# Row-group pairs of score and maxima products in a two-layer gated attention kernel, with gathers and scatters issued one at a time in the first half of a step

## The reference

```python
x = x + tanh(g_xattn[0]) * L0_xattn(layernorm(x), ctx, mask1)   # no biases but bo, mask per (query, key)
x = x + tanh(g_ffn[0])   * L0_ffn(layernorm(x))                 # 8 experts, the best 2 of each row, exact gelu
x = x + tanh(g_xattn[1]) * L1_xattn(layernorm(x), ctx, ctx, mask2)  # with biases
x = x + tanh(g_ffn[1])   * L1_ffn(layernorm(x))                 # fft, sparse complex product, ifft, bias
```

## Time and profile before

| | us |
|---|---|
| median of 3 executions | 1349.95 |
| lowest, highest | 1343.78, 1759.76 |
| the profiled execution | 1340.18, span 1338.6, mean granted clock 0.944 |

### The profile page before, as it was taken

How to read it: one execution, slowest core, us unless ns; L and a number is a source line. 1 busy time by engine, 2 the same in 40 slices (tenths; PEclk the granted TensorE clock), 3 DMA queues, 4 the chain that set the end, 5 groups by cost and what they waited for, 6 DMA issues and landing times.

```text
span 1338.6 us, 35030 instructions
## 1 busy us (share of the span) xinstructions
PE 1210.1 (90%) x11816; PEld 1001.9 (75%) x11816; DVE 890.7 (67%) x2695; ACT 570.9 (43%) x1187; POOL 261.6 (20%) x374
## 2 busy tenths in 40 slices
PE   4898999988869999899998999999997999999996
PEld 3777777777658888688886888888874777777784
DVE  4787767777647675565856676766565777777763
ACT  4565555545423232422324242422233555555462
POOL 5024334233320000000000000000022334433310
PEclk9998978878779999999999999999997999999998
DMA  9544324334434021131301212101122222222200
GB/s 294 169 129 145 125 89 139 105 113 152 153 127 147 32 92 59 48 105 36 126 31 59 95 56 88 40 29 37 39 65 66 64 72 87 77 75 70 86 29 24
DMA packets 82755, 119.67 MB, mean 89 GB/s; under 512 B 27325, under 2 KB 52557, under 8 KB 80588
## 3 DMA queue, kind: packets, MB, share of 16 engines
q1 hardware_dynamic: 64172, 60.32, 14.6%
q0 software_dynamic: 12848, 49.05, 11.2%
q10 hardware_dynamic: 5616, 8.78, 1.8%
HBM read 63.81 MB, written 47.58 MB: 83 GB/s over the span
## 4 chain that ended last, share of the span: by engine, by line
PE 77%; DVE 8%; issue 7%; ACT 2%; SPq 2%; ACTq 2%; DMA 1%; POOL 0%; DVEq 0%; POOLq 0%; another core or an unknown queue 0%
PE bank L1758 25%; PE bank L1771 13%; PE bank L1519 7%; PE bank L1585 7%; PE bank L1441 5%; PE bank L1572 3%; PE bank L1504 3%; PE bank L1502 3%; PE bank L1461 3%; PE bank L1525 2%; PE bank L1596 1%; PE bank L1545 1%; PE bank L1583 1%; DVE bm L1081 1%; PE bank L1487 1%
## 5 line engine op out<-in xcount | busy, mean ns | idle before, releaser
L1758 PE MATMUL bank<-tiles,we 128*128 128x256 f16 (+1 forms) x3744 | 395.3, 259 | 5.9 <-issue 5.0
L1758 PEld LDWEIGHTS bank<-tiles,we 128*128 128x128 f16 x3744 | 326.1, 98 | 47.5 <-issue 13.5
L935 ACT ACTIVATE tiles<-bank 128x256 f32<-128x256 f32 (+1 forms) x312 | 109.5, 354 | 336.0 <-PE bank L1758 302.5
L1771 PE MATMUL bank<-we,tiles 128*128 128x256 f16 x1608 | 224.8, 274 | 20.9 <-DVE tiles L1372 20.0
L1368 DVE SCALAR_TENSOR_TENSOR tiles<-bank,tiles 128x256 f32<-128x256 f32 (+1 forms) x312 | 120.1, 385 | 165.7 <-ACT tiles L935 161.6
L1771 PEld LDWEIGHTS bank<-we,tiles 128*128 128x128 f16 x1608 | 148.2, 98 | 58.3 <-DVE tiles L1372 33.7
L1081 DVE TENSOR_REDUCE bm<-bank 128x4 bf16<-128x308 f32 x256 | 116.5, 475 | 78.7 <-PE bank L1504 62.9
L1519 PE MATMUL bank<-qT,kbd 128*128 128x256 f16 x960 | 166.7, 294 | 2.4 <-issue 1.4
L471 DVE TENSOR_TENSOR pr<-pr 128x512 f16<-128x512 f32 x160 | 108.5, 682 | 35.2 <-ACT pr L797 32.7
L1374 DVE TENSOR_TENSOR tiles<-tiles 128x256 f16<-128x256 f32 (+1 forms) x312 | 121.1, 388 | 12.1 <-DVE tiles L1372 1.7
L1519 PEld LDWEIGHTS bank<-qT,kbd 128*128 128x128 f16 x960 | 99.1, 106 | 24.8 <-issue 3.0
(11 more groups left out here) (197 smaller groups left out, 1693.3 us busy)
## 6 DMA issues: line engine op xcount, KB each, us to landing
expert_out<-zeros SPq DMA_DIRECT2D x16, 896.0 KB
wes<-in_guT POOLq DMA_DIRECT2D x9, 1024.0 KB, 5.1
tiles<-expert_in SPq DMA_DIRECT2D x29, 256.0 KB, 2.6
pr<-in_guT POOLq DMA_DIRECT2D x7, 1024.0 KB
yg<-in_dnT POOLq DMA_DIRECT2D x7, 1024.0 KB
expert_out<-tiles ACTq DMA_DIRECT2D x28, 256.0 KB, 2.1
expert_in<-zeros POOLq DMA_DIRECT2D x8, 640.0 KB, 12.8
xin<-in_x SPq DMA_DIRECT2D x16, 256.0 KB
```

What stands on the lines that cost most here:

```text
L935: act.activation(ge[:, fc % 2, 0:n * P], bank[1 + fc % 3][:, 0:n * P], ACT.Gelu, scale=INV).then_inc(s.gelu, 1)
L1758: last = pe.matmul(bank[1 + fc % 3][:, half * S:half * S + w * P], gate_up[:, par, c, i, col:col + P], xT[:, j, c, 0:w * P], start=n == 0, ...
L1771: last = pe.matmul(bank[4 + t][:, 0:D], act16[:, fc % 4, i, t * P:(t + 1) * P], we[:, par, 2, j, fc * D:(fc + 1) * D], start=fc == 0 and n ...
```

## The change

Chunks: the 616 columns of a half are cut so that chunks 0 and 1 hold columns 0 to 255 (heads 0 to 3, partitions 0 to 63), chunks 2 and 3 columns 360 to 615 (heads 4 to 7, partitions 64 to 127), and `REST` the columns 256 to 359, which cross. Group 0 is the two rest chunks at full height (`scores_rest`). Groups 1 and 2 (half c=0), and 3 and 4 (c=1), are made together: four mask products first, then the key products two by two, one on partitions 0 to 63 for one group and one on 64 to 127 for the other, into different banks. The maxima products likewise go in pairs (`top_pair`), over four banks instead of two. The exponentials read two banks at once. The order of all queues is rewritten: TensorE has all scores before `values`, ACT all exponentials before `q_hi`, DVE `w_low(b, 1)` ahead of `residual` and `w_low` 3 and 4 ahead of the maxima. The scatters handle batch b-3 instead of b-2; scatter or gather 0 follows the mask copy, 1 and 2 the copy `a_hi`, 3 the first root. `recall` comes one step earlier, at the step's end, for which `slots` gets a 17th column. The number of matrix products and of transfers is the same.

```diff
+REST = 4
+CHUNKS = (0, P, ROWS - 2 * P, ROWS - P, (ROWS - P) // 2)
 NCH = len(CHUNKS)
 GS = KC * NCH // 2
+GROUPS = (((0, REST), (1, REST)), ((0, 0), (0, 1)), ((0, 2), (0, 3)), ((1, 0), (1, 1)), ((1, 2), (1, 3)))
 NW = 8
...
-        bank = [ctx.enter_context(nc.psum_tensor(f"bank{i}", [P, 512], F32)) for i in range(8)]
+        banks = [ctx.enter_context(nc.psum_tensor(f"bank{i}", [P, 2, 512], F32)) for i in range(4)]
+        bank = [banks[i // 2][:, i % 2] for i in range(8)]
...
-        def a_place(g):
-            return b_top[:, 0:4 * S2] if g % 2 == 0 else b_small[:, 0:4 * S2]
+        def a_place(b, g):
+            if isinstance(b.i, int) and b.i == 0:
+                return bank[(5, 2)[g % 2]][:, 0:4 * S2]
+            return bank[(5, 2, 3, 4)[g % 4]][:, 0:4 * S2]
...
+        def score_place(g, j):
+            if g == 0:
+                return bank[3][:, j * S:(j + 1) * S]
+            return banks[(0, 2, 3, 1, 2)[g]][:, j, 0:S]
...
-                late = b.layer == 0 and not (isinstance(b.i, int) and b.i < 2)
+                late = b.layer == 0 and not (isinstance(b.i, int) and b.i < 3)
+                part = ld and b.layer == 1
+                one = (lambda n: gather(b.after(3), n)) if part else (lambda n: scatter(b.after(-3), n))
+                if part:
+                    wait_apart(pool, s.places_recalled, b.i + 4)
+                if late:
+                    scatter_ready(b.after(-3))
+                if late or part:
+                    wait_apart(pool, s.mask_ready, b.n + 1)
+                    one(0)
+                    if tail:
+                        wait_apart(pool, s.attended_high, pv.n + 1)
+                    one(1)
+                    one(2)
                 if tail:
                     ln_root(1, s.root_after, s.variance_after, pv)
+                if late or part:
+                    one(3)
                 if pre:
                     root(b.after(2))
-                if ld and b.layer == 1:
-                    gather(b.after(3))
-                if late:
-                    for t in range(QT):
-                        scatter(b.after(-2), t)
+                if b.layer == 0 and isinstance(b.i, int) and b.i == 15:
+                    scatter_ready(b.after(-2))
+                    for n in range(2 * QT):
+                        scatter(b.after(-2), n)
...
+                expo(b, 0)
                 if tail:
                     a_hi(pv)
-                expo(b, 0)
                 expo(b, 1)
+                expo(b, 2)
                 if front:
                     h_hi(nx)
-                expo(b, 2)
                 expo(b, 3)
+                expo(b, 4)
                 if front:
                     q_hi(nx)
                 if tail:
...
                     v_spread(nx, 0)
                 if tail:
                     tail_out(pv)
-                expo(b, 4)
...
-                if ld and b.layer == 1:
-                    recall(b.after(3))
                 if pre and b.layer == 0:
                     mask_flags(b.after(2))
                 w_low(b, 0)
+                w_low(b, 1)
                 if tail:
                     residual(pv)
-                w_low(b, 1)
                 w_low(b, 2)
                 if b.layer == 0 and not (isinstance(b.i, int) and b.i < 2):
                     place(b.after(-2))
...
                     renorm(pv)
                 if pre:
                     pre_stats(b.after(2))
+                w_low(b, 3)
+                w_low(b, 4)
                 if front:
-                    q_low(nx)
                     maxima(nx, 0)
                     maxima(nx, 1)
+                    q_low(nx)
                     maxima(nx, 2)
                     maxima(nx, 3)
-                w_low(b, 3)
-                if front:
-                    maxima(nx, 4)
                 if pre:
                     pre_norm(b.after(2))
                 if front:
+                    maxima(nx, 4)
                     maxima(nx, 5)
-                w_low(b, 4)
-                if front:
                     maxima(nx, 6)
                     maxima(nx, 7)
                 if tail:
...
                         route(pv, 0)
                     else:
                         finish(pv)
+                if ld and b.layer == 1:
+                    recall(b.after(4))
                 normalise(b)
...
+            def top_pair(b, k):
+                t, c = k // KC, k % KC
+                if k == 0:
+                    pe.wait_ge(s.queries_high, b.n + 1)
+                    pe.wait_ge(s_kbd[b.par], 16 * HC * (b.half + 1))
+                    pe.wait_ge(s.mask_ready, b.n)
+                elif k > 1:
+                    pe.wait_ge(s.maxima, b.n * GP + 2 * (k - 1))
+                for u in range(2):
+                    pe.matmul(a_place(b, 2 * k + u), identb[:],
+                              bm[:, t, 0:S2].unsqueeze(1).to_broadcast([P, 4, S2]), start=True, stop=False)
+                for u in range(2):
+                    rows64 = slice(u * 64, (u + 1) * 64)
+                    last = pe.matmul(a_place(b, 2 * k + u), qT[rows64, b.par, 0, c, t * P:(t + 1) * P],
+                                     kbd[rows64, b.par, 0, c, 4 * u:4 * u + 4], start=False, stop=True)
+                    last.then_inc(s.top_scores, 1)
...
+            def score_keys(b, ki, c, chunk):
+                flat = kbd[:, b.par, ki, c].rearrange("p h k -> p (h k)")[:, CHUNKS[chunk]:CHUNKS[chunk] + P]
+                return flat if chunk == REST else flat[chunk // 2 * 64:chunk // 2 * 64 + 64]
+            def masked(g, j, start):
+                c, chunk = GROUPS[g][j]
+                first = c * ROWS + CHUNKS[chunk]
+                keys = mhead[:].rearrange("p h k -> p (h k)")[:, first:first + P]
+                return pe.matmul(score_place(g, j), keys, mrhs[:], start=start, stop=not start)
+            def scores_rest(b):
+                pe.wait_ge(s.queries_low, b.n + 1)
+                pe.wait_ge(s_kbd[b.par], 16 * HC * (b.half + 1))
+                for j in range(2):
+                    c = GROUPS[0][j][0]
                     for n, (ki, qi) in enumerate(PASSES):
+                        pe.matmul(score_place(0, j), score_keys(b, ki, c, REST), qT[:, b.par, qi, c],
+                                  start=n == 0, stop=False)
+                    if j == 0:
+                        pe.wait_ge(s.mask_ready, b.n + 1)
+                    last = masked(0, j, False)
+                last.then_inc(s.scores, 1)
+            def scores(b, c):
+                g = 1 + 2 * c
+                if c == 0:
+                    if isinstance(b.i, int) and b.i == 0:
+                        pe.wait_ge(s.bulk_low, NU * (b.layer + 1))
+                else:
+                    pe.wait_ge(s.weights, b.n * GS + 2)
                 for j in range(2):
+                    for u in range(2):
+                        masked(g + u, j, True)
+                for j in range(2):
+                    for n, (ki, qi) in enumerate(PASSES):
+                        for u in range(2):
+                            rows64 = slice(u * 64, (u + 1) * 64)
+                            last = pe.matmul(score_place(g + u, j), score_keys(b, ki, c, 2 * u + j),
+                                             qT[rows64, b.par, qi, c], start=False, stop=n == 2)
+                            if j == 1 and n == 2:
+                                last.then_inc(s.scores, 1)
...
-                    pe.wait_ge(s.values_spread, KC * b.n + 1)
-                    if isinstance(b.i, int) and b.i == 0:
-                        pe.wait_ge(s.bulk_low, NU * (b.layer + 1))
+                    pe.wait_ge(s.values_spread, KC * b.n + 2)
+                    pe.wait_ge(s.weights, b.n * GS + 3)
...
                 nx, pv = b.after(1), b.after(-1)
+                scores_rest(b)
+                if tail:
+                    t_att(pv)
                 scores(b, 0)
-                if tail:
-                    pe.wait_ge(s.values_spread, KC * b.n + 2)
-                    t_att(pv)
-                scores(b, 1)
                 if tail:
                     if not (isinstance(pv.i, int) and pv.i < 1):
...
                         pe.wait_ge(s.bias_rows_in, 16)
                     proj_o(pv)
                 if front:
-                    if not tail:
-                        pe.wait_ge(s.values_spread, KC * b.n + 2)
+                    pe.wait_ge(s.values_spread, KC * b.n + 2)
                     t_h(nx)
-                scores(b, 2)
-                scores(b, 3)
+                scores(b, 1)
                 ranked = b.layer == 0 and not (isinstance(b.i, int) and b.i < 2)
                 if front:
                     if tail:
...
                     prefix(b.after(-2))
                 if front:
                     proj_q(nx)
-                scores(b, 4)
                 if ranked:
                     pe.wait_ge(s.ranks_read, b.i - 1)
                 if front:
                     spread(nx, 0)
```

(23 more changed lines are left out.)

102 lines of the change are left out of this document (42 added, 60 removed).

## The result

| | before | after |
|---|---|---|
| median, us | 1346.87 (4 executions) | 1360.3 (4, 1358.07 to 1365.39) |
| the profiled execution's span, us | 1338.6 | 1359.5 |
| layer 0, 15 steps between first and last mask copy | 297.5 | 339.2 |
| from there to layer 1's first mask copy (experts) | 681.3 | 686.1 |
| layer 1, 15 steps | 284.1 | 254.6 |

The changed kernel is slower by a little: 1.011 times the time before, 95% interval 1.0078 to 1.0143. One of the four executions of before took 1759.76 us, and the ratio leaves it out. I had forecast 1323. The two layers went opposite ways: layer 0 lost 42 us where I had it gain 12, layer 1 gained 29 where I had 15. The set-up ahead of the first mask copy took 4 us more.

A forecast was written before the change was run, and what follows sets the result against it. Bound: a loop from output projection through residual, statistics, root, maxima and mask copy to next scores. Layer 1 15 us, layer 0 10 and 2, together 27 off the 1350 median: 1323, own range 1300 to 1335, over all cases 1292 to 1370.

The forecast's parts named there:

- The new wait in layer 0: ACT's norm of batch b-1 waits for all four scatters of b-3; layer 0 step 18.05 us at full clock.
- the landing: Layer 0's fourth scatter, issued behind POOL's root, lands 1.9 to 2.0 us after its start, at +11.3 instead of +9.4.
- the slow stretch of 6.8 us: Layer 0 runs 6.8 us of each step at 1.2 GHz; charged 2.4 us a step, the same as before.
- rival 3: TensorE with fewer columns falls to 1.2 GHz more often: layer 1 loses 20 us, layer 0 16; 1386 us, chance 0.16.
- rival 1: Pairing works, but scatter wait and clock hold layer 0 at 20.4 us; only layer 1's 15 us gained, 1335, chance 0.25.
- My walk: Layer 1's step followed queue by queue from the mask copy: next one at +17.9 us against 18.98, 1.05 less.
- the price of one stream: A pair of half-height score or maxima products costs what one did, freeing 1.8 us of TensorE per step.
- rival 2: Each change between full and half height empties TensorE, eating the pairing's gain; 1350 to 1357 us, chance 0.17 with pairs in series.
- DVE without idle time: Sign: DVE becomes the next bound, its queue without a gap between the second norm's shift and the last maxima.
- The clock of layer 1: Layer 1 keeps its full granted clock; below 1.00 would be the sign of the clock rival, rival 3.
- the gathers at no cost: Layer 1's gathers are needed only at the step's end or by later steps, so moving them early costs nothing.
- the case to which I gave 0.18: The changed kernel is slower than before by more than the two per cent, 27 us, that a measurement can tell.

The follow-up runs named there:

- clear_early: Changed kernel with SP issuing the 896 KB clear near the start of its step instead of last; 1296.2 us, ratio 1.0331.
- before_new_pool: Kernel before with only the moved transfers and the recall one step earlier, no pairs, no other order; 1327.2 us, ratio 1.0592.
- before_scatter4_early: before_new_pool with the fourth transfer issued right behind the third, ahead of POOL's root; 1270.8 us, ratio 1.0128.
- after_again: Changed kernel, unchanged, run again on another chip; 1349.6 us, ratio 1.077 to the kernel before on that chip.
- full_height: scatter4_early with every score and maxima product on 128 rows again, queue orders and banks kept; 1283.2 us, ratio 1.0211.
- scatter4_early: Changed kernel with the fourth scatter and gather issued right behind the third, ahead of POOL's root; 1277.8 us, ratio 1.0203.

## Why the prediction was wrong

**The new wait in layer 0: right place, wrong size.** I named ACT's norm behind the fourth scatter, and that is where it waits, 13 times. The term that failed is the landing: 1.9 to 2.0 us after its start, taken from one scatter that ran with little beside it. It was 4.4 and more, and most of the excess is SP's clear of 896 KB, issued 0.6 us ahead of it: with the clear elsewhere (clear_early) the landing took 2.6 us, and the norm waited 2.0 to 2.3 us in the steps without a fetch of weights, where I had it 1.9. I had looked at what stands in POOL's queue, and not at what SP issues at the new place.

**What the clock made of it.** I charged the slow stretch of 6.8 us as it was and called the sum 20.4, then took 19.8. The stretches at a granted clock of 0.50 became 10.2 to 13.7 us, one in each step with the wait. That is the second step of the prediction that failed, an overlap: I took the clock's price as the same with the new wait as without it. The wait of TensorE stands directly before its small maxima and logit products (the eight logit products took 1.87 us at half clock), and the granted clock fell while TensorE stood. That is the price of rival 3, in layer 0 alone (layer 1 stayed at 1.00), but not for its reason: it is set off by the wait that rival 1 names. before_new_pool streams the columns of the kernel before and has stretches of 6.8 us or more in most steps, before_scatter4_early has none in its steady steps. On the other chip the step was 16.25 us at full clock and went to 21.6 to 24.2, of which the wait itself is 4.3; with the wait at 2.0 to 2.3 (clear_early) it was 18.1 to 19.4 with one stretch of 6.8 us in every second step. I had treated rivals 1 and 3 as apart; the one brings on the other. Layer 0's steps with scatters were forecast 0.8 us faster and were 3.6 slower (24.1 against 20.5 on average over 12), 43 us; the first three gave 1.6 back.

**Layer 1: 1.05 forecast, 1.82 measured, for other reasons.** The step went from 18.97 to 17.16 in the first comparison, yet from 17.28 to 17.15 on another chip. So most of the first number is not the pairs; it belongs to what slowed the kernel before in the first comparison, of which the late starts are the part that can be seen. My walk compared itself with that trace's step, which holds 1.12 us of late start at this one place. It was there to be seen: ACT's wait of 2.74 us is put down to a product whose end lay 1.12 us back, and TensorE then stood 0.81 us.

**Pairs: price right, gain halved by the changes of mode.** Pairs run together at the price of one stream; that step held. I then gave TensorE 1.8 us per step free and let DVE take over as the bound at 17.9. The drain of rival 2 is there too, some 0.1 us at each change where I had priced 0.16 to 0.19: the two score islands save 0.92 us of TensorE (0.75 of the step), the four maxima pairs lose 0.24 (0.22 of the step), and the new order costs 0.41. The Trainium skill (TensorEngine Tiling (Array Packing), "Key Properties") says that changing the tiling mode drains the engine; the traces agree, at about 0.1 us a change. "DVE without idle time" was wrong: it waits 1.15 us for the root and 1.30 for the last maxima. The clock of layer 1 and the gathers at no cost were right.

**The sum.** -15 and -10 and -2 were forecast. Measured between the profiled executions: layer 1 -29.5, layer 0 +41.7, experts +4.8, set-up +4.2, end -0.3, in all +20.9. The time lay inside my range of 1292 to 1370 and within the two per cent of no change to which I gave 0.42, but on the slow side of before and 37 us above my 1323; on the other chip the change costs 7.7%, the case to which I gave 0.18. Of the case that came, a scatter wait that draws the clock down, I had two halves and no sum. The least sure term, the landing, would have changed the sign: with 4.4 instead of 2.0 us my own walk has layer 0 at 20.4 + 2.4 = 22.8, 2.2 above 20.6, and the total at 1350 - 15 - 2 + 13 x 2.2 = 1362. That this is 2 us from the measured time is luck: this walk has layer 1 gain 15 where it gained 29.5, and layer 0 lose 27 where it lost 42.

**Slips in the working.** None of them changes the forecast. From 212.4 to 219.0 are 6.6 us; the 6.8 used is what the windows give, with the fall at about 212.1. The steps of DVE's walk in layer 1 add up to +12.9 where it says +13.1. Layer 0 at 18.05 would be three times its forecast gain, not twice.

## What to carry to other kernels

A transfer that something waits for is priced with what the other queues issue in the same microseconds, not by the quietest one in the trace; and where TensorE waits for it ahead of small products, look for a second price in the granted clock. Row-group pairs pay only where the stream they save is longer than two changes of mode, here about 0.2 us: an island of twelve products of 256 columns gained 0.46 us, one pair of 308 columns lost 0.06. Before a walk is made from a trace, look for waits whose named releaser had ended long before: such time may belong to the run and not to the program.

## What the runs showed of the hardware

A scatter of 128 rows landed 4.4 to 4.9 us after its start with a clear of 896 KB issued 0.6 us ahead of it (after, after_again), and 2.6 us after it with the clear elsewhere (clear_early). A change between products on 128 and on 64 rows took about 0.1 us (full_height and scatter4_early). With a wait of 3.3 us of TensorE in a step the granted clock was at 0.50 for 10.2 to 13.7 us of it (after). The same program took 1347 us in one comparison and 1253 to 1255 on three other chips, and in the slower one ACT started its copy of TensorE's turned rows 0.4 to 2.0 us late in 24 of 32 steps; the cause is open.
